# Last layer of a four-layer graph network: the order of three steps on ScalarE and of three on VectorE changed

## The reference, cut to what matters

```python
def _L3_gnn_ref(x, adj, weight, bias):
    deg = jnp.maximum(adj.sum(axis=1, keepdims=True), 1e-08)
    w = adj / deg
    log_ij = _logmap(x[:, None, :], x[None, :, :], c)
    agg = jnp.einsum('ij,ijc->ic', w, log_ij)
    transformed = agg @ weight + bias
    return _expmap(jnp.zeros_like(transformed), transformed, c)
```

## Time and profile before

| | |
|---|---|
| median of 3 runs | 1581.26 us (1580.57 to 1583.12) |
| the profiled execution, its own time | 1582.32 us |
| its span, first to last instruction | 1580.5 us |
| granted TensorE clock, mean | 0.940 |
| busy: TensorE, VectorE, ScalarE, GpSimd | 1392.8, 1235.0, 930.4, 213.2 us |
| the 72 units of the last layer | about 1118 to 1531 us |

### The profile page before, as it was taken

One profiled execution on the slowest core, in us unless ns is written; L12 is line 12 of the kernel. 1 busy time (PEld: TensorE's weight loads), 2 busy tenths in 40 slices (PEclk: granted clock), 3 DMA queues, 4 the chain that ended last, 5 costly groups with the idle time before them and its releaser, 6 DMA issues. The chain is left out here.

```text
span 1580.5 us, 20433 instructions
## 1 busy us (share of the span) xinstructions
PE 1392.8 (88%) x7857; PEld 603.8 (38%) x7882; DVE 1235.0 (78%) x1623; ACT 930.4 (59%) x888; POOL 213.2 (13%) x145
## 2 busy tenths in 40 slices
PE   4999999789978699999999999979988898888870
PEld 1433333223324244454454454534433333333330
DVE  4899866676785877968969958528688878999877
ACT  0000286358633555445456456766879989989964
POOL 1000000000000000000000001223224444444430
PEclk9999999999997799999999999989869989999995
DMA  9999599979999255434434432234534546455600
GB/s 332 409 409 409 233 407 410 413 286 409 409 414 411 76 189 216 179 134 181 180 120 180 184 117 67 79 108 158 176 103 137 179 150 204 148 181 179 213 15 27
DMA packets 135896, 348.93 MB, mean 221 GB/s; under 512 B 7732, under 2 KB 57208, under 8 KB 135544
## 3 DMA queue, kind: packets, MB, share of 16 engines
q1 hardware_dynamic: 119968, 329.27, 56.0%
q10 hardware_dynamic: 15832, 18.36, 3.3%
HBM read 329.78 MB, written 17.83 MB: 220 GB/s over the span
## 5 line engine op out<-in xcount | busy, mean ns | idle before, releaser
L955 PE MATMUL ps<-ring,X 128*64 128x512 f32 x512 | 263.8, 597 | 15.2 <-DVE ring L2149 15.2
L956 PE MATMUL ps<-work,X 128*64 128x512 f32 x512 | 263.8, 597 | 0.0
L1471 ACT ACTIVATE work<-ring 128x2048 f32<-128x2048 f32 x64 | 122.3, 1911 | 156.4 <-PE ps L963 122.9
L963 PE MATMUL ps<-work 128*64 128x512 bf16 x768 | 208.2, 380 | 0.0
L961 PE MATMUL ps<-work 128*64 128x512 bf16 x768 | 208.2, 380 | 0.0
L727 POOL TENSOR_TENSOR ring<-ring,work 128x1024 f32<-128x1024 f32 x72 | 170.8, 2372 | 247.7 <-DVE work L2406 247.7
L824 PE MATMUL ps<-ring,work 128*64 128x512 f32 x672 | 159.5, 620 | 20.7 <-DMA ring<-in_adjT 20.7
L720 POOL TENSOR_SCALAR work<-ring 128x1024 int16<-128x1024 uint8 x24 | 27.0, 1127 | 1031.8 <-DMA ring<-codes 930.7
L961 PEld LDWEIGHTS ps<-work 128*64 128x64 bf16 x768 | 84.7, 110 | 177.4 <-issue 151.9
L1131 PE MATMUL ps<-ident,work 128*128 128x128 f32 x448 | 79.8, 305 | 52.5 <-DVE work L2338 26.0
L1297 ACT ACTIVATE work<-work,code_bias 128x2048 uint8<-128x2048 bf16 (+1 forms) x32 | 62.3, 1947 | 90.6 <-DVE work L1892 80.2
(11 more groups left out here) (365 smaller groups left out, 2847.2 us busy)
## 6 DMA issues: line engine op xcount, KB each, us to landing
ring<-in_adjT SPq DMA_DIRECT2D x88, 2048.0 KB, 15.9
work<-in_adjT SPq DMA_DIRECT2D x28, 2048.0 KB, 20.0
ring<-in_adjT SPq DMA_DIRECT2D x24, 1024.0 KB, 9.7
ring<-in_adjT SPq DMA_DIRECT2D x48, 512.0 KB, 3.8
ring<-codes SPq DMA_DIRECT2D x32, 512.0 KB, 3.7
ring<-in_adjT SPq DMA_DIRECT2D x64, 256.0 KB, 3.0
codes<-work ACTq DMA_DIRECT2D x32, 256.0 KB, 6.1
codes<-work ACTq DMA_DIRECT2D x64, 128.0 KB, 1.8
```

The source lines that it names most:

```text
L955: nc.tensor.matmul(ps[0:F, h, :], rows, ring[:, r, k, cols], start=start, stop=stop)
L956: nc.tensor.matmul(ps[F:P, h, :], rows, negs[:, pair, i, cols], start=start, stop=stop)
L963: mm = nc.tensor.matmul(ps[F:P, 2 + h, :], part, less[:, pair, i, cols], start=start and t == 0, stop=stop and t == 2)
L1471: nc.scalar.activation(negs[:, pair], ring[:, s % RING, 2 * pair:2 * pair + 2, :], ACT.Relu, scale=-1.0).then_inc(negs_made, 1)
```

## The change

On ScalarE, period n becomes: Ln(n), raise(n+1), root(n), angle(n-1), inverse(n). On VectorE: product(n+1), sum(n), mirror 0 of n-2, weight(n-1), mirror 1 of n-2. No instruction is added or removed and none changes its operands or its semaphores; TensorE, GpSimd and the DMA queue keep their order.

```diff
--- before.py
+++ after.py
@@ -1610,15 +1610,13 @@
 
             raise_dist(units[0])
             for n in range(LAST_PERIOD):
-                v = unit_at(n - 1)
-                if v:
-                    act.wait_ge(sum_made, v.n + 1)
-                    nc.scalar.activation(v.angle, v.angle, ACT.Ln, scale=2.0 / DIST_SCALE).then_inc(
-                        angle_made, 1)
-                u = unit_at(n)
+                u, v = unit_at(n), unit_at(n - 1)
                 if u:
                     act.wait_ge(prod_made, u.n + 1)
                     nc.scalar.activation(u.log, u.log, ACT.Ln, bias=TINY_PROD, scale=1.0).then_inc(log_made, 1)
+                if unit_at(n + 1):
+                    raise_dist(units[n + 1])
+                if u:
                     if u.n >= 3:
                         act.wait_ge(weighted, u.n - 2)
                         w = units[u.n - 3]
@@ -1626,10 +1624,11 @@
                             act.wait_ge(g_turned, 2 * w.offs + 2)
                     act.wait_ge(log_made, u.n + 1)
                     nc.scalar.activation(u.angle, u.log, ACT.Exp, scale=0.5).then_inc(root_made, 1)
+                if v:
+                    act.wait_ge(sum_made, v.n + 1)
+                    nc.scalar.activation(v.angle, v.angle, ACT.Ln, scale=2.0 / DIST_SCALE).then_inc(angle_made, 1)
                 if n == 0:
                     copy_nodes(2)
-                if unit_at(n + 1):
-                    raise_dist(units[n + 1])
                 if n == FLIPS_OUT_AT[2]:
                     copy_signs(3)
                 if n == 5:
@@ -2399,13 +2398,8 @@
                 if n - 1 in products_end[:-1]:
                     quad = products_end.index(n - 1)
                     add_mirror(quad, units[quad_ends[quad]])
-                v = unit_at(n - 1)
-                if v:
-                    dve.wait_ge(angle_made, v.n + 1)
-                    dve.wait_ge(inv_made, v.n + 1)
-                    V.scalar_tensor_tensor(v.angle, v.angle, ANGLE_CLIP, v.log, ALU.min, ALU.mult).then_inc(g_made, 1)
-                if turned_at(n - 2):
-                    mirror_weights(units[n - 2], 0)
+                if unit_at(n + 1):
+                    multiply(units[n + 1])
                 u = unit_at(n)
                 if u:
                     dve.wait_ge(root_made, u.n + 1)
@@ -2415,9 +2409,14 @@
                 if n == 0:
                     copy_nodes(2)
                 if turned_at(n - 2):
+                    mirror_weights(units[n - 2], 0)
+                v = unit_at(n - 1)
+                if v:
+                    dve.wait_ge(angle_made, v.n + 1)
+                    dve.wait_ge(inv_made, v.n + 1)
+                    V.scalar_tensor_tensor(v.angle, v.angle, ANGLE_CLIP, v.log, ALU.min, ALU.mult).then_inc(g_made, 1)
+                if turned_at(n - 2):
                     mirror_weights(units[n - 2], 1)
-                if unit_at(n + 1):
-                    multiply(units[n + 1])
                 if n == 0:
                     copy_sums2(NQ - 1)
                 if n == 2:
```

## The result

The changed kernel takes **1899.2 us** (median of 4 runs, 1895.5 to 1902.2) against 1580.9 (4 runs), a ratio of 1.2015 with a 95% interval of 1.1983 to 1.2046: 318 us slower. The forecast was 1867, range 1750 to 1990. The profiled execution took 1900.4 us, its span is 1898.3.

A forecast was written before the change was run, and what follows sets the result against it. A loop of waits through several engines was taken to bound the last layer, 5.25 us per quiet period. 1582.3 + 182 (171 + 5 + 6, full clock) + 103 (clock) = 1867 us, range 1750 to 1990.

The forecast's parts named there:

- The loop: Last layer: product, sum, mirror 0, TensorE's pass, distances, raise, product span one period, not two; 8.81 us between O units.
- The clock: TensorE in the last layer: 1.2 GHz in part of every period, granted clock taken as 0.71, +103 us.
- Rival 2: Last layer: loop closed, TensorE's clock nearly full, 1764 us; chance 0.08.
- rival 3: Last layer: loop closed, TensorE almost always at 1.2 GHz, about 1983 us; chance 0.11.
- the 171: Last layer, 68 periods at full clock: the closed loop takes 552.6 us against 381.2 before, +171 us.
- the 5: TensorE, ahead of push and distances: halves of `move_x` and `turn_last_nodes` now on the path, about 5 us.
- VectorE's way: Periods without mirror products: the way by mirror 0, weight and mirror 1 on VectorE is the longer, 8.08 us.
- rival 1: Last layer: loop closed, clock mixed, 1867 us, 1800 to 1940 for granted clock 0.90 to 0.60; chance 0.72.
- The tail: From last product to last addition: 11.3 us before, about 17 with the new order, +6 us.
- the first periods: Periods 0 to 2 of the last layer: bound by layer 2's end on TensorE, left alone in the forecast.
- VectorE's small work: Adding up sums, keeping moved rows, norm steps: costs nothing beside the product; at most 25 us if that cover failed.
- Rivals 4 and 5: Last layer: loop doesn't close, 1548 us, chance 0.05; only part holds, some step overlaps more, 1600 to 1740 us, chance 0.04.

The follow-up runs named there:

- its two variants: The kernel before with product and mirror 1 exchanged on VectorE, 1599.0 us; the kernel before with 5 matmuls added on TensorE in 11 periods, 1591.8 us.

## Why the prediction was right, point by point

**The loop.** Right in its place, its steps and its length. At full clock (8 matmuls added, or the single periods that had it) the kinds of period measure 8.82 (forecast 8.81), 8.16 (8.08), 9.70 (9.78), 8.24 (8.23), 7.37 (7.26); behind a D 6.90 (6.87), in periods without mirror products in that run, and in one with four chunks in the changed kernel. These short sums leave out the periods that also move rows or outlast the added work. That TensorE's unchanged order closes the loop is shown from both sides: the product alone brings the loss, earlier distances take most of it away.

**The clock.** Right in kind, and the assumed 0.71 was 0.73 over the last layer. That it costs is shown: with 57 of the 68 periods at full clock 90 us of these periods came back. Rival 2 (1764, clock full) and rival 3 (1983, clock always low) did not happen. The Trainium skill's "TensorE: Matmul & The Clock Gate" (section "HAM oscillation — how this bites in real kernels") says that each burst behind a long wait starts cold, and that agrees with the rows; that the whole burst stays cold, as rival 3 had it, it does not say of bursts as long as these, and in the O period shown only the first two groups and a part of the third are.

**The term that was mis-sized** is the clock's price. I had +279 us for the 68 periods (171 + 5 + 103); they measure +305. With the 171 and the 5 as forecast, the clock cost 129 us and not 103. The step that was too cheap is dividing TensorE's time on the path by the mean clock of a stretch: that mean counts the idle time too. In the O period shown above the clock is 0.83, by which the division gives 4.75 / 0.83 - 4.75 = 0.97 us, and the period is 1.52 us longer than 8.81. In the O periods the forecast is met all the same, 8.81 + 1.94 = 10.75 against 10.66, but in part by luck: their clock was 0.78 and not 0.71. The short periods show the error. In the ten turned periods without mirror products I took VectorE's way, 8.08, with 2.28 us of TensorE in it, in all about 9.0; they take 10.42, at a clock of 0.66. At 1.2 GHz TensorE's own way (two transpositions and the gather) becomes the longer. The 14 periods behind a D take 8.5 instead of 7.8 at a clock of 0.71, the seven next to one without mirror products 9.5 instead of 8.6 at 0.65, the six with two chunks 10.4 instead of 9.9. Together that is 14 + 10 + 6 + 3 us, less 2 in the O periods, 31 us: the 26 that are missing, and the 5 forecast for the halves of `move_x` and `turn_last_nodes`, which stand in these periods.

One sum of the prediction is off by 8 us: 1764 + 252 / 0.90 - 252 is 1792 and 1764 + 252 / 0.60 - 252 is 1932, where rival 1 says 1800 to 1940. The measured 1899 lies inside either.

**The small terms.** The tail was +8.3 (forecast 6), the first periods +4.5 (forecast none); VectorE's small work is hidden in the wait for the raise, as forecast.

**Rivals 4 and 5** fell with the loop. The change does remove the 30 us wait of the sum, but no measured run turned that into a gain: with the distances early and GpSimd's work cut down it still takes 1617 us.

## What to carry to other kernels

When an instruction moves forward on one engine, follow what it waits for back through the orders of the other engines, to the instruction of its own engine that this needs: if that one now stands in the same period, a loop that spanned two periods spans one, and its whole length is the period. Do it for every wait that the new order meets, not for the one in question; a loop that I left out made one expectation wrong by 190 us, and another is part of a miss of 37. And price a matmul on such a path at the clock of the rows behind a like idle time, not at the stretch's mean.

## What the runs showed of the hardware

**VectorE stands still behind GpSimd, and GpSimd behind VectorE.** A product with both inputs in SBUF that starts while GpSimd's multiplication runs ends 1.08 to 1.09 us after it, in all 173 products over 1.3 us of six runs (the kernel before, its two variants, and the runs with the weight, ScalarE's order or the distances moved). It takes up to 3.0 us instead of 1.22; with only the weight moved the mean was 2.5 us at GpSimd's full work and 1.22 with its work cut to an eighth. The other way round holds too. In 15 periods of the run with only the weight moved GpSimd starts 0.16 us after a product, and then it takes 3.27 us instead of 2.35:

```profile
1294.28 1.22 DVE L2328 SCALAR_TENSOR_TENSOR work<-work 128x1024 f32<-128x1024 f32 x1
1294.44 3.27 POOL L727 TENSOR_TENSOR ring<-ring,work 128x1024 f32<-128x1024 f32 x1 [5.81 <-DVE work L2416]
```

The Trainium skill says so ("SBUF — State Buffer", section "SBUF: two separate sides": a VectorE instruction with two SBUF inputs and a GpSimd instruction that reads SBUF exclude each other for a whole instruction), and these runs agree. The sum and the mirrors, which read PSUM and at most one SBUF operand, keep their 1.22 and 0.68 us beside GpSimd (the earlier trace rows with the GpSimd row at 1511.80).

**Work added to TensorE can shorten a kernel.** Eight useless matmuls in each idle time, 3.5 of 4.1 us filled, raised the granted clock from 0.74 to 1.00 and saved 93 us. Cutting the gather's work lowered it from 0.73 to 0.66, and an O period became only 0.3 us shorter. In the kernel before, where each of these idle times was shorter than the five matmuls put there, they cost 10.5 us.
